# Cross attentions of two decoder layers without the identity products that TensorE ran in their gaps

## The chip, the cores and the metric

The kernel runs on one core of a Trainium2 chip. The metric is the device time of one execution in microseconds. A core has five engines that run side by side and meet at semaphores: TensorE (matrix products into PSUM; its weight loads are a lane of their own in the profile), VectorE, ScalarE, GpSimd and SyncE (which issues the DMAs). TensorE's clock is granted at one of two levels, 2.4 and 1.2 GHz; the profile shows it as a share, 1.00 or 0.50.

## The reference, cut to what matters

The program is a decoder of four layers, each with a mixing sublayer, a cross attention and a feed-forward sublayer, on x of 4 sequences x 512 tokens x 128. The two layers in question have the same cross attention, with 16 heads of width 8 over a context of 77 rows:

```python
q = query @ Wq.T + bq                      # query = layernorm(x)
k = key @ Wk.T + bk                        # key = value = context, 77 rows
v = value @ Wv.T + bv
attn = einsum('bhqd,bhkd->bhqk', q, k) / sqrt(8)
attn = softmax(attn, axis=-1)
out = einsum('bhqk,bhkd->bhqd', attn, v)
x = x + (out @ Wo.T + bo)
```

## The kernel before, in words

A loop of two passes takes two sequences each. A pass has twelve stages in a fixed order (`STAGES`), each run for the first sequence and then for the second, every one a block of its own in which each engine has a written-out list of instructions; engines meet at the block's end. So the cross attention is built four times (`stage_l0_xattn`, `stage_l1_xattn`, two sequences each) and executed eight times. Layer 0's follows a linear attention and is followed by an expert layer (`experts_stage` with weighed outputs); layer 1's follows a causal attention and is followed by another expert layer. While a stage works on one sequence it also does pieces of the norm of the other one (`m.side`): adding the last result to the residual, mean and variance on VectorE, a transpose on TensorE.

`cross_attention_stage` for one sequence: TensorE makes keys (L609), queries (L610) and values (L611). ScalarE adds biases, VectorE spreads the keys over four head groups. The score products (L624) come in four groups of 128 tokens, four row quarters of the array at a time; VectorE takes the maximum of each group (L715), and from the third on a score group waits for the banks that a maximum has freed. The negated maxima, split into two bf16 parts, are transposed on TensorE (L631), copied by ScalarE (L681), and added to scores made anew the other way round: per head group g, `shifted(g)` makes products of keys and queries (L640) and adds the shift (L645), ScalarE takes the exponential of all of it (L686), and `mix(g)` multiplies with the values and with ones (L654). TensorE's order is shifted(0), shifted(1), mix(0), shifted(2), mix(1), shifted(3), mix(2), the side's transpose, mix(3). VectorE then takes the reciprocals of the sums (L730) and multiplies (L732), in two halves, and TensorE projects each half (L671).

In five places of this list TensorE runs identity products before it waits: `m.warm(pe, count, bank)` multiplies the bf16 identity with four copies of itself (L97, 128x128 by 128x512) into a bank that nothing has yet to read. These are six before the scores, ten before the transposes of the maxima, ten before shifted(1), ten before the first half of the projection, four before the second: 40 in a stage. Other stages have such products of their own (the expert layer of layer 0 has 36 before its gates are transposed).

Of the kernel before, what the change touches and what calls it, by code (L numbers as in the profile page):

```python
# [560 lines left out]
def cross_attention_stage(m, name, w):  # L561
# [6 lines left out]
    with ExitStack() as ctx:  # L568
# [33 lines left out]
        with nc.Block(no_gpsimd_drain=True) as block:  # L602
            @block.sync
            def _(sync):
                m.housekeeping(sync)

            @block.tensor
            def _(pe):
                pe.matmul(m.psum[:, 5, 0:S2], w["wk"], m.ctxT[:, :], start=True, stop=True).then_inc(qkv_psum, 1)  # L609
                pe.matmul(m.bank(4), w["wq"], m.xnT[:, :], start=True, stop=True).then_inc(qkv_psum, 1)  # L610
                pe.matmul(m.psum[0:S2, 6, 0:D], m.ctxT[:, :], w["wv"], start=True,  # L611
                          stop=True).then_inc(qkv_psum, 1)
                m.warm(pe, 6, 0)
                pe.wait_ge(q_ready, 1)
                pe.wait_ge(k_of_ready, 1)
                for t in range(NT):
                    base = 4 * (t % 2)
                    if t == 1:
                        pe.wait_ge(v_ready, 2)
                        m.side.released(pe)  # L620
                    if t >= 2:
                        pe.wait_ge(peak_ready, t - 1)
                    for r in range(R):
                        ins = pe.matmul(m.psum[:, base + r, 0:G * S2], qT[quad(r), t * P:(t + 1) * P],  # L624
                                        k_of[quad(r), :, :].rearrange("p g s -> p (g s)"), start=True, stop=True)
                    ins.then_inc(scores_ready, 1)
                pe.wait_ge(peak_ready, NT - 1)
                m.warm(pe, 10, 0)
                pe.wait_ge(shift_ready, 1)
                for t in range(NT):  # L630
                    ins = pe.transpose(m.psum[:, 4, t * P:(t + 1) * P],  # L631
                                       shift[:, t, :, :].rearrange("p r w -> p (r w)"), m.ident)
                ins.then_inc(shift_psum, 1)

                def shifted(g):
                    if g >= 1:
                        m.warm(pe, 10 if g == 1 else 0, 4)
                        pe.wait_ge(exps_ready, g)
                    for r in range(R):
                        pe.matmul(m.psum[0:S2, r, :], k_of[quad(r), g, :], qT[quad(r), :], start=True, stop=False)  # L640
                    if g == 0:
                        pe.wait_ge(shiftT_ready, 1)
                        pe.wait_ge(cleared, 2)
                    for r in range(R):
                        ins = pe.matmul(m.psum[0:S2, r, :], pick[quad(r), g, :], shiftT[quad(r), :], start=False,  # L645
                                        stop=True)
                    ins.then_inc(shifted_psum, 1)

                def mix(g):
                    pe.wait_ge(exps_ready, g + 1)  # L650
                    for n in range(2):
                        for r in range(R):
                            lhsT = v[:, 4 * r + g, :] if n == 0 else m.const["ones_of"][0:S2, g, :]
                            ins = pe.matmul(m.psum[quad(r), 5 + n, :], lhsT, prob[:, g % 2, r, :], start=g == 0,  # L654
                                            stop=g == G - 1, skip_group_check=True)
                    ins.then_inc(group_mixed, 1)

                for g in range(G + 1):
                    if g < G:
                        shifted(g)  # L660
                    if g >= 1:
                        mix(g - 1)
                    if g == G - 1:
                        pe.wait_ge(peak_ready, NT)
                        m.side.turn(pe, [m.psum[:, OUT, t * P:(t + 1) * P] for t in range(NT)])
                for half in range(2):
                    m.warm(pe, 4 if half else 10, 4)
                    pe.wait_ge(mixed_ready, half + 1)
                    m.side.taken(pe)
                    for t in (2 * half, 2 * half + 1):  # L670
                        pe.matmul(m.psum[:, OUT, t * P:(t + 1) * P], mixed[:, t * P:(t + 1) * P], w["wo"],  # L671
                                  start=t == 0, stop=True, skip_group_check=True)
# [3207 lines left out]
```

## Time and profile before

| | us |
|---|---|
| median of three executions | 4097.55 (4093.26 to 4102.58) |
| the profiled execution | 4104.73 |
| its span, first to last instruction | 4103.0 |
| TensorE busy with products, in the span | 3673.0 (90%), 37500 of them |
| identity products among them (L97) | 1304, busy 323.2 |
| VectorE busy | 2470.9 (60%) |
| ScalarE busy | 1540.4 (38%) |
| mean granted clock of TensorE | 0.957 |

Matmuls are pipelined and overlap in the rows, so that ten of them can take less time than ten times the duration of one. A row of the timeline has the start, the time taken, the engine (PE is TensorE's products, PEld its weight loads, DVE is VectorE, ACT is ScalarE), the line of the kernel, the operation, what it writes and reads, the shape, the count, and in brackets the idle time before it and what ended it. f32 products are listed twice each.

### The profile page before, as it was taken

Reading aid. Unit: us, or ns where it says so; the run is one execution under the profiler, and the core shown is the slowest. Engines: PE = TensorE matmul, PEld = TensorE weight load, DVE = VectorE, ACT = ScalarE, POOL = GpSimd, SP = SyncE. Lnnn points to the kernel's source line nnn. Section 1 sums busy time; section 2 is a strip of 40 time slices with the busy share of each in tenths; the row PEclk is TensorE's granted clock in tenths of the full one; section 3 lists DMA queues with packets and bytes.
Section 4 is the critical chain, followed back from the end, with each engine's and each line's share of the span. In section 5 each row is a group of like instructions: output and inputs, shape, how many; then the busy total and the mean of one; then the engine's idle time right before and its main releaser. Section 6 shows DMA issues by size and latency. Waiting matters only on the chain. (4 is left out here: it accounts for less than half of the span.)

```text
span 4103.0 us, 93379 instructions
## 1 busy us (share of the span) xinstructions
PE 3673.0 (90%) x37500; PEld 2356.3 (57%) x37500; DVE 2470.9 (60%) x5994; ACT 1540.4 (38%) x3558; POOL 883.9 (22%) x1564
## 2 busy tenths in 40 slices
PE   6998999988898889999979989999888988999999
PEld 3886886433354336665548868864333544466655
DVE  6677676566435676555466676765665356765454
ACT  4445444233222335432244454432332222345322
POOL 1441441011001203320024414410110011133100
PEclk9999999999999999899989999999999999989999
DMA  2000000010000000010010000000100000000100
GB/s 95 3 3 2 3 3 13 1 54 1 21 1 20 1 25 2 1 41 18 12 35 3 3 1 3 3 13 1 54 1 21 1 20 1 26 1 1 41 29 6
DMA packets 8676, 59.92 MB, mean 15 GB/s; under 512 B 893, under 2 KB 5297, under 8 KB 5937
## 3 DMA queue, kind: packets, MB, share of 16 engines
q1 hardware_dynamic: 8240, 53.86, 3.4%
q8 instruction: 304, 4.98, 0.5%
q14 instruction: 132, 1.07, 0.1%
HBM read 52.81 MB, written 1.05 MB: 13 GB/s over the span
## 5 line engine op out<-in xcount | busy, mean ns | idle before, releaser
L97 PE MATMUL psum<-ident_bf 128*128 128x512 bf16 x1304 | 323.2, 393 | 15.3 <-PEq L2566 4.0
L3113 ACT ACTIVATE l_attn_ax<-psum 128x128 f32<-128x128 f32 (+1 forms) x768 | 186.4, 278 | 397.0 <-PE psum L2928 276.8
L3352 DVE TENSOR_TENSOR l_attn_xx<-l_attn_xx,psum 128x256 f32<-128x256 f32 x512 | 205.0, 419 | 214.2 <-PE psum L2947 203.1
L438 ACT ACTIVATE l_ffn_silu<-psum 128x512 f32<-128x512 f32 (+2 forms) x208 | 124.1, 597 | 469.5 <-PE psum L404 415.0
L503 DVE TENSOR_TENSOR l_ffn_hidden<-l_ffn_silu,psum 128x512 f32<-128x512 f32 (+2 forms) x176 | 120.5, 687 | 283.6 <-ACT l_ffn_silu L438 283.6
L103 PEld LDWEIGHTS psum<-streamed_weights,l_ffn_hidden 128*128 128x128 f32 (+2 forms) x1664 | 215.4, 192 | 123.0 <-issue 112.3
L2943 PE MATMUL psum<-l_attn_ax,l_attn_xx 64*64 64x64 f32 x5120 | 272.0, 226 | 0.0
L2947 PE MATMUL psum<-l_attn_xx,l_attn_ax 64*64 64x64 f32 x5120 | 263.9, 223 | 0.0
L3239 POOL TENSOR_TENSOR l_attn_part<-l_attn_ab,streamed_weights 128x128 f32<-128x128 f32 x640 | 245.4, 414 | 39.4 <-PE psum L2928 20.3
L103 PE MATMUL psum<-streamed_weights,l_ffn_hidden 128*128 128x128 f32 (+2 forms) x1664 | 224.2, 278 | 14.1 <-DVE l_ffn_hidden L503 9.2
L97 PEld LDWEIGHTS psum<-ident_bf 128*128 128x128 bf16 x1304 | 126.3, 103 | 183.0 <-issue 50.1
L2943 PEld LDWEIGHTS psum<-l_attn_ax,l_attn_xx 64*64 64x64 f32 x5120 | 211.3, 140 | 17.7 <-issue 10.2
L2928 PE MATMUL psum<-l_attn_xx,l_attn_part 64*64 64x64 f32 x5120 | 205.7, 231 | 8.1 <-DVE l_attn_xx L3352 6.3
L936 DVE TENSOR_REDUCE l_attn_peak<-psum 128x4 f32<-128x2048 f32 (+3 forms) x128 | 182.6, 1484 | 47.0 <-PE psum L862 46.6
L2947 PEld LDWEIGHTS psum<-l_attn_xx,l_attn_ax 64*64 64x64 f32 x5120 | 210.5, 139 | 0.0
L2928 PEld LDWEIGHTS psum<-l_attn_xx,l_attn_part 64*64 64x64 f32 x5120 | 183.8, 142 | 36.6 <-issue 17.4
L904 ACT ACTIVATE l_attn_prob<-psum 128x1024 f32<-128x1024 f32 (+1 forms) x192 | 159.9, 882 | 76.9 <-DVE l_attn_total L946 42.4
L859 PE MATMUL psum<-l_attn_k,l_attn_q 32*128 32x512 f32 (+3 forms) x1024 | 117.2, 530 | 71.5 <-DVE l_attn_peak L936 57.7
L2721 DVE SCALAR_TENSOR_TENSOR l_attn_conv<-psum,streamed_weights,l_attn_conv 128x511 f32<-128x511 f32 (+2 forms) x192 | 140.7, 747 | 16.3 <-ACT l_attn_conv L2661 11.8
L403 PE MATMUL psum<-l_ffn_gated_x,streamed_weights 128*128 128x512 f32 x256 | 139.3, 626 | 5.9 <-DVE l_ffn_gated_x L482 5.9
L3218 POOL TENSOR_TENSOR l_attn_pm<-l_attn_pm,w_const 128x256 f32<-128x256 f32 x128 | 93.0, 730 | 210.6 <-DVE l_attn_pm L3279 210.6
L813 PE MATMUL psum<-l_attn_q,l_attn_k 32*128 32x512 f32 (+3 forms) x1024 | 102.9, 473 | 38.2 <-ACT l_attn_prob L904 38.2
(541 smaller groups left out, 7858.7 us busy)
## 6 DMA issues: line engine op xcount, KB each, us to landing
streamed_weights<-pack_l_ffn SPq DMA_DIRECT2D x2, 5284.0 KB, 15.3
streamed_weights<-pack_l_attn SPq DMA_DIRECT2D x3, 2848.5 KB, 9.6
streamed_weights<-pack_l_ffn SPq DMA_DIRECT2D x2, 3972.0 KB, 13.0
streamed_weights<-pack_l_xattn SPq DMA_DIRECT2D x2, 2496.0 KB, 9.4
streamed_weights<-pack_l_ffn SPq DMA_DIRECT2D x2, 2192.0 KB, 8.1
streamed_weights<-pack_l_xattn SPq DMA_DIRECT2D x2, 2048.0 KB, 8.8
streamed_weights<-pack_l_ffn SPq DMA_DIRECT2D x2, 1923.0 KB, 7.9
streamed_weights<-pack_l_attn SPq DMA_DIRECT2D x2, 1091.5 KB, 5.1
```

The source lines that it names most:

```text
L97: pe.matmul(self.bank(bank), self.ident_bf[:, :], self.ident_bf[:, :].unsqueeze(1).to_broadcast([P, NT, P]), start=True, stop=True)
L103: ins = pe.matmul(self.psum[:, OUT, t * P:(t + 1) * P], features[:, t * P:(t + 1) * P], weight, start=first and t == 0, stop=last, skip_gr ...
L403: pe.matmul(m.bank(n % 2)[0:r], w["up"][:, c:c + r], rhs, start=True, stop=True)
L904: act.activation(prob[:, u % SLOTS, 2 * half:2 * half + 2, 0:used(part)], m.psum[:, base:base + 2, 0:used(part)], ACT.Exp).then_inc(exps_r ...
L936: dve.tensor_reduce(peak[:, g, i, :], m.psum[:, base:base + R, 0:(i + 1) * P], AX, ALU.max, negate=True).then_inc(peak_ready, 1)
L2721: ins = dve.scalar_tensor_tensor(out=later, in0=m.psum[:, chunk_bank(n), 0:T - 3 + i], scalar=w["conv_w"][:, ORDER[n], i:i + 1], in1=later ...
L2928: ins = pe.matmul(m.psum[b, p, W * i:W * i + W], part[b, (M * n + l - 1) % 2, p, i, :], xx[b, n % 2, p, X, i, :], start=True, stop=True)
L2943: pe.matmul(m.psum[b, p, P + W * i:P + W * i + W], xx[b, n % 2, p, XT, i, :], ax[b, p, i, :], start=True, stop=True)
L2947: ins = pe.matmul(m.psum[b, p, 256 + W * i:256 + W * i + W], ax[b, p, i, :], xx[b, n % 2, p, XT, i, :], start=True, stop=True)
L3113: act.activation(ax[b, p, :, :], m.psum[b, p, 0:P].rearrange("p (i t) -> p i t", i=2), ACT.Copy).then_inc(ax_ready, 1)
L3239: pool.tensor_tensor(part[:, q % 2, p, :, :], ab[:, n % 2, p, :, 0:W], over_block(w["levels"][:, l, :]), ALU.mult).then_inc(part_ready, 1)
L3352: dve.tensor_tensor(both, both, m.psum[:, p, P:384], ALU.subtract).then_inc(x_less, 1)
```

## The change

Four calls of `warm` go from `cross_attention_stage`, which stand for five groups of products in each stage (the last call is in a loop of two). All other instructions, their order and their waits stay. The identity products of the other stages stay.

```diff
                 pe.matmul(m.psum[0:S2, 6, 0:D], m.ctxT[:, :], w["wv"], start=True,
                           stop=True).then_inc(qkv_psum, 1)
-                m.warm(pe, 6, 0)
                 pe.wait_ge(q_ready, 1)
                 pe.wait_ge(k_of_ready, 1)
...
                 pe.wait_ge(peak_ready, NT - 1)
-                m.warm(pe, 10, 0)
                 pe.wait_ge(shift_ready, 1)
...
                 def shifted(g):
                     if g >= 1:
-                        m.warm(pe, 10 if g == 1 else 0, 4)
                         pe.wait_ge(exps_ready, g)
...
                 for half in range(2):
-                    m.warm(pe, 4 if half else 10, 4)
                     pe.wait_ge(mixed_ready, half + 1)
                     m.side.taken(pe)
```

## Rows read from the trace of the kernel before

**Rows 1.** Head of the page.

```profile
span 4103.0 us, 93379 instructions
```

**Rows 2.** Stretches, L97 alone: from:to us, PE and PEld busy (count), clock, DMA.

```profile
715.10:748.30 33.20, 10.95 (x40) 4.03 (x40) 0.95 0.00 0
...
3117.30:3149.10 31.80, 9.48 (x40) 3.66 (x40) 1.00 0.01 1
```

**Rows 3.** Timeline of TensorE's two lanes, layer 0, second sequence, first pass.

```profile
716.48 1.46 PE L97 MATMUL psum<-ident_bf 128*128 128x512 bf16 x6
717.87 0.83 PEld L624 LDWEIGHTS psum<-l_xattn_k_of,l_xattn_qT 32*128 32x128 f32 x16 [0.42 <-issue]
722.93 3.80 PE L97 MATMUL psum<-ident_bf 128*128 128x512 bf16 x10 [0.55 <-DVE l_xattn_peak L715]
726.35 0.58 PEld L631 LDWEIGHTS psum<-w_const,l_xattn_shift 128*128 128x128 f32 x4
730.60 0.23 PEld L640 LDWEIGHTS psum<-l_xattn_qT,l_xattn_k_of 32*77 32x77 f32 x8 [0.42 <-ACT l_xattn_prob L686]
747.24 0.71 PE L671 MATMUL psum<-w_l_xattn,l_xattn_mixed 128*128 128x128 f32 x4 [0.55 <-DVE l_xattn_mixed L732]
```

**Rows 4.** Timeline of ScalarE and VectorE in the same stage.

```profile
716.46 0.69 ACT L679 ACTIVATE l_xattn_qT<-psum,w_l_xattn 128x512 f32<-128x512 f32 x1 [0.58 <-PE psum L610]
...
724.59 0.22 DVE L723 TENSOR_TENSOR l_xattn_shift<-l_xattn_peak,l_xattn_coarse 128x64 f32<-128x64 f32 x1
...
728.45 1.87 ACT L686 ACTIVATE l_xattn_prob<-psum 77x2048 f32<-77x2048 f32 x1 [0.65 <-PE psum L645]
731.96 1.87 ACT L686 ACTIVATE l_xattn_prob<-psum 77x2048 f32<-77x2048 f32 x1 [1.64 <-PE psum L645]
```

**Rows 5.** Stretches, TensorE: from:to us, PE busy (count), clock, DMA.

```profile
719.20:722.40 3.20, 1.60 (x16) 1.00 0.00 0
722.60:725.90 3.30, 2.97 (x8) 0.50 0.00 0
...
730.60:742.70 12.10, 11.87 (x105) 1.00 0.00 0
...
865.90:876.10 10.20, 9.91 (x61) 0.50 0.01 2
```

**Rows 6.** Timeline, begin of layer 1's stage, first sequence, first pass.

```profile
1039.29 0.42 PE L609 MATMUL psum<-ctxT,w_l_xattn 128*128 128x77 f32 x2 [0.42 <-PEq L792]
...
1043.74 1.32 PE L624 MATMUL psum<-l_xattn_k_of,l_xattn_qT 32*128 32x308 f32 x16
...
1041.15 0.69 ACT L679 ACTIVATE l_xattn_qT<-psum,w_l_xattn 128x512 f32<-128x512 f32 x1 [1.08 <-PE psum L610]
```

**Rows 7.** Timeline of TensorE in the causal attention, clock at either level.

```profile
864.44 1.14 PE L859 MATMUL psum<-l_attn_k,l_attn_q 32*128 32x512 f32 x8 [3.02 <-PEq L1000]
...
871.38 2.09 PE L859 MATMUL psum<-l_attn_k,l_attn_q 32*128 32x512 f32 x8
...
893.37 1.97 PE L800 MATMUL psum<-w_const,l_attn_shift 128*128 128x128 f32 x8 [0.30 <-DVE l_attn_peak L936]
...
897.19 0.66 PE L800 MATMUL psum<-w_const,l_attn_shift 128*128 128x128 f32 x4
```

**Rows 8.** Timeline, layer 0, first sequence: what precedes the first exponentials.

```profile
694.08 1.28 ACT L686 ACT_TABLE_LOAD   x1
694.11 0.12 PEld L645 LDWEIGHTS psum<-l_xattn_shiftT,l_xattn_pick 32*77 32x77 bf16 x4 [0.53 <-ACT l_xattn_shiftT L681]
694.28 0.39 PE L645 MATMUL psum<-l_xattn_shiftT,l_xattn_pick 32*77 32x512 bf16 x4
```

**Rows 9.** Timeline, begin of the expert layers after the second sequences.

```profile
752.47 8.31 PE L97 MATMUL psum<-ident_bf 128*128 128x512 bf16 x36
...
759.38 0.36 DVE L475 TENSOR_TENSOR l_ffn_gate<-l_ffn_work,l_ffn_parts 128x192 f32<-128x192 f32 x1
...
1111.74 1.13 PE L103 MATMUL psum<-streamed_weights,l_ffn_hidden 128*128 128x128 f32 x8 [0.91 <-DVE l_ffn_hidden L503]
```

## The prediction, made before the changed kernel was run

> **What bounds the kernel now.** I read the page first: 4103.0 us from first to last instruction [rows 1]; the profiled execution took 4104.73 us, so 1.73 us lie around the span, and it stands 7.2 us above the median of the runs, 4097.55. Then I read the eight cross attentions that the change touches: two layers, two sequences each, in a loop of two passes. I call them A1 and A2 (layer 0, first and second sequence), B1 and B2 (layer 1). Each takes about 33.3 us and issues 40 products of the identity with itself (L97), 320 in all [rows 2]; in A2 they fill 10.95 of 33.2 us of TensorE.
>
> The timelines of TensorE, VectorE and ScalarE over A2 show what each of the five groups stands in front of [rows 3, 4]. Group 1 (six) stands before the score products: the queries are there at 717.15 (716.46 plus 0.69), the scores' first weight load comes at 717.87. Group 2 (ten) stands before the transposes: the shifts are there at 724.81, the transposes' load comes at 726.35. Group 3 (ten) stands before the second head group: the first exponentials end at 730.32, the load comes at 730.60. Groups 4 and 5 (ten and four) stand before the two halves of the output projection; the row at 747.24 has an idle 0.55 us before it that VectorE's division ended, so there VectorE sets the time and the products cost nothing.
>
> So in each stage one chain runs through queries, scores, four maxima on VectorE, transposes, ScalarE's exponentials, mixing, reciprocals. TensorE lies on it in short pieces, and how long these take depends on the granted clock. That is the last view: stretches with the clock. In the mixing loop the clock is at 2.4 GHz (1.00), TensorE busy 11.87 of 12.10 us [rows 5]. In A2 it fell to 1.2 GHz (0.50) right after the later score groups, when TensorE had been busy 1.60 of 3.20 us, and was back while group 2 ran [rows 5]. Five of the eight stages show that fall in the middle; both B1 show one at their begin instead; the last B2 shows none and is 31.8 us long, about 1.5 us shorter than A2 [rows 2].
>
> **What goes, by the waits alone.** A released weight load follows within 0.05 us: in A1 at 694.11, where ScalarE, done with what it waited for, had gone on at 694.08 [rows 8].
> - Group 1: 717.87 less 717.20 is 0.67 us; alike in six stages. In B1, where the group ran at 1.2 GHz, the scores come at 1043.74 and the queries were there at 1041.84 [rows 6]: 1.86, and 1.92 in the second pass. Together 7.8 us.
> - Group 2: 726.35 less 724.87 is 1.48 in A2 (twice); the same difference is 0.94 and 0.91 in A1, 1.60 in the first B2, and nothing in the three stages where the group ran at full clock. Together 6.4 us.
> - Group 3: ScalarE waits 1.64 us between first and second exponentials [rows 4] and 1.41 between the later ones: 0.23 in six stages, nothing in A1, where an activation table is loaded before the first exponentials [rows 8]. Together 1.4 us.
> - Groups 4 and 5: nothing.
>
> The sum is 15.6 us, if nothing else changes.
>
> **What it costs.** The groups are the only work of TensorE in these gaps. Without them A2 has, after its first two score groups, two groups of 0.8 us, then 2.5 us idle (722.38 to 724.87), then transposes and first shifted scores, then 1.9 us idle until the exponentials are through. The clock fell already after 719.2 to 722.4, where the score groups stand with gaps of 1.04 and 0.55 us; what follows them after the change is emptier. So I take it that transposes and shifted scores run at 1.2 GHz in every stage, and that the mixing loop begins so. At the end, with two gaps (2.35 us from 742.77 to 745.12, and 1.4) around four short products, I take the clock to fall too, and the next stage to begin at 1.2 GHz.
>
> Prices, from rows at either level [rows 7]: eight score products of 512 columns take 1.14 us at 2.4 GHz and 2.09 at 1.2; four transposes 0.66, against 0.99 (1.97 for eight); ten identity products 3.80, most of them at half clock [rows 3], against 2.33 at full clock in the same stage.
> - Transposes to first exponentials: 2.10 us now (726.35 to 728.45). Colder by 0.33 for the transposes, 0.95 for L640, and about 0.37 for L645 (0.39 at full clock): 1.65 us in six stages, 9.9. In A1 the table load ends at 695.36, 0.7 us after L645 (694.67), and hides that much [rows 8]: 0.95 twice, 1.9.
> - Mixing loop: at full clock TensorE has 0.2 us to spare in 12.1, so it is the bound as soon as its work doubles, and a cold stretch costs half its length. Stretches at 1.2 GHz are from 3.3 us (722.6 to 725.9) to 10.2 (865.9 to 876.1) long [rows 5]. I take 4.7 us, nearer to the short one, as the loop leaves TensorE no idle time once it is the bound: 2.35 us times eight, 18.8. Bounds 1.7 and 5.1 each, 13 and 41 together.
> - Begin of A2 and B2: L609 and L610 to the queries take 2.04 us at full clock and 2.55 in B1, where the clock fell soon after the begin [rows 6]; at half clock throughout up to 3.3. So 0.5 to 1.3 more; I take 1.0, and 0.6 for the first score group (0.87 from its load to the first maximum): 1.6 times four, 6.4. In B1, cold already, 0.6 twice, 1.2.
> - Maxima: a later score group, 0.8 us, takes about 1.4 at half clock, which just fits under a maximum of that length; 0.15 in each stage, 1.2.
> - The second half of the projection at half clock, on the way to the stage's end: 0.71 becomes 1.05, by the transposes' ratio, as these are products of 128 columns too; eight times, 2.8.
> - The expert layers that follow A2 and B2 begin colder. In the first the 36 identity products that stay end after the gates are ready (752.47 plus 8.31 is 760.78; the gates end at 759.74 [rows 9]), so a delay there shows: 0.8 twice. In the second TensorE has 0.91 us of idle before its first down projection [rows 9], against some 4 us of products that slow down: 1.7 twice. Together 5.0; bounds nothing and 10.
>
> The costs make 9.9 + 1.9 + 18.8 + 6.4 + 1.2 + 1.2 + 2.8 + 5.0 = 47.2 us; less 15.6 is 31.6 us slower. On the profiled execution that is 4136.3; on the median of the runs **4129 us**.
>
> Nothing is added or moved: no DMA, no wait, no buffer. The banks that the groups wrote (0 and 4) are written again from a fresh start by what follows.
>
> **A rule of the skill, against the rows.** The clock fell in A2 after gaps of 1.04 and 0.55 us between bursts, not after a long idle stretch. The Trainium skill (TensorE: Matmul & The Clock Gate, "Why this matters for your kernels") asks only that no long idle gap stand between bursts of matmuls, and none of the gaps that stay here is as long as it names. By that rule the clock would not fall and the change would give the 15.6 us; it is the first rival, and the rows of five stages speak against it.
>
> **Rivals.**
> - Waits alone (12 in 100; the other side): the clock stays at 2.4 GHz, or falls only where it falls now. Its place is the gap before the transposes, its price the 15.6 us: 4082 us. For it: the last B2, where the clock never fell [rows 2]. Against it: there too the score groups ended in identity products, which now go. It decides if the clock at the transposes is 1.00 in most stages.
> - A short fall (12 in 100): the clock falls before the transposes, is back before the mixing loop, and stages begin at full clock. Then 9.9 + 1.9 + 1.2 stand against 15.6: 2.6 faster, 4095, that is no change. For it: in A2 it was back after 3.3 us. Against it: it came back under dense identity products, and now the exponentials leave TensorE idle there.
> - A long fall (14 in 100): the loop, which keeps the clock at 2.4 GHz now, doesn't soon bring it back once it begins at 1.2. One more stretch of 3.4 us per loop adds 8 times 1.7: 4143; the whole loop at half clock costs some 11.9 us in place of 2.35: 8 times 9.5 more, 4205. For it: 865.9 to 876.1, 9.91 of 10.20 us busy and still at 0.50.
>
> **How the numbers follow.** My forecast has 62 in 100; its own range is 4112 to 4150: down by 6 for the loop's lower bound and by some 11 for the stage begins and expert layers, up by 22 for the loop's upper one. With the rivals the range is 4092 to 4160: waits alone lies below, the worst of the long fall above. A change of under 0.2% (8 us) can't be told from none here. Faster by more: 0.15 (waits alone, part of the short fall); the same: 0.10; slower: 0.75.
>
> **What would show it.** Right: in the changed profile the clock is 0.50 from before the transposes into the mixing loop in nearly every stage; L640's eight products near 2 us there; exponentials one to two 1.5 us later than 1.41; A2 and B2 begin at 0.50; each stage some 3 to 5 us longer. Scores start 0.05 us after the queries and transposes 0.05 us after the shifts, whatever the clock. Wrong: the clock 1.00 through the loop and stages of about 31 us; or all the loss after the stages, in the expert layers, which I price lowest.

## The result, and the profile after

The changed kernel took 4142.34 us (median of three executions, 4142.20 to 4143.18), the kernel before, beside it, 4100.07: a ratio of 1.0105, with a 95% interval of 1.0085 to 1.0125. A fourth execution took 9095.90 us, at a mean granted clock of 1.00; it is left out of these figures, and nothing here shows its cause. A second comparison gave 1.0077 (1.0059 to 1.0094): 4141.26 against 4110.29. The two differ in the kernel before (4100.07 and 4110.29), hardly in the changed one. The change makes the kernel slower by some 31 to 43 us. The forecast was 31.6 slower, 4129 us with a range of 4112 to 4150; the measured time lies in that range, in its upper part.

The heads of the page after: span [rows 1], busy time of the engines, and the identity products that are left.

```profile
span 4141.5 us, 92747 instructions
...
PE 3655.9 (88%) x37180; PEld 2338.9 (56%) x37180; DVE 2473.0 (60%) x5994; ACT 1539.5 (37%) x3558; POOL 883.8 (21%) x1564
...
L97 PE MATMUL psum<-ident_bf 128*128 128x512 bf16 x984 | 238.7, 387 | 11.9 <-PEq L2562 4.0
```

The span is 38.5 us longer, with 320 products fewer. I cut both traces at the first instruction of each stage (VectorE's addition to the residual) to see where. The eight cross-attention stages are 31.7 us longer together (3.4 to 5.7 each), the four expert layers that follow A2 and B2, in their first sequence, 11.1 (2.0 twice, 2.7, 4.4), and all the rest is 4.3 shorter, in pieces of up to 3 us of either sign in stages that nothing was changed in. One part of that rest is regular: the second sequences of the same expert layers are 1.6 to 1.9 us shorter each, 6.8 together, so that the expert layers as a whole lose 4.3.

Within A2 the granted clock answers to [rows 2, 5]. TensorE's stretches after the change: from:to us, length, PE busy (count), clock, DMA share, GB/s.

```profile
689.30:706.30 17.00, 12.51 (x60) 0.50 0.00 0
...
716.60:723.40 6.80, 4.80 (x15) 0.50 0.00 0
723.50:730.10 6.60, 2.44 (x32) 1.00 0.00 0
730.30:733.60 3.30, 3.21 (x16) 0.50 0.00 0
733.70:737.00 3.30, 1.52 (x16) 1.00 0.00 0
737.10:743.80 6.70, 6.70 (x36) 0.50 0.01 2
743.90:754.00 10.10, 7.37 (x64) 1.00 0.00 0
754.20:764.30 10.10, 8.86 (x22) 0.50 0.00 0
```

The first row is A1, from the transposes into the mixing loop; the others run through A2, from before its begin to the expert layer. In A2 the clock is at 1.2 GHz four times: over the begin, at the transposes, inside the loop, and at the end. Ahead of the last three falls TensorE had stood idle for part of a stretch at 2.4 GHz: it was busy 2.44 of 6.60 us, 1.52 of 3.30, 7.37 of 10.10. The loop, which ran at full clock from its first product [rows 5], spends 6.7 us at half.

TensorE's timeline over A2 [rows 3] shows what that makes of the instructions: start us, us, line, operands, count, and the idle time before with what ended it.

```profile
717.83 1.22 PE L667 MATMUL psum<-w_l_xattn,l_xattn_mixed 128*128 128x128 f32 x4 [1.41 <-DVE l_xattn_mixed L728]
...
719.94 2.00 PE L610 MATMUL psum<-xnT,w_l_xattn 128*128 128x512 f32 x2
...
722.72 1.62 PE L623 MATMUL psum<-l_xattn_k_of,l_xattn_qT 32*128 32x308 f32 x16 [0.35 <-ACT l_xattn_qT L675]
...
730.13 1.02 PE L629 MATMUL psum<-w_const,l_xattn_shift 128*128 128x128 f32 x4 [2.58 <-DVE l_xattn_shift L719]
731.08 2.00 PE L637 MATMUL psum<-l_xattn_qT,l_xattn_k_of 32*77 32x512 f32 x8
...
735.48 1.10 PE L637 MATMUL psum<-l_xattn_qT,l_xattn_k_of 32*77 32x512 f32 x8 [1.97 <-ACT l_xattn_prob L682]
...
738.15 1.95 PE L651 MATMUL psum<-l_xattn_prob,w_const 77*32 77x512 f32 x8
740.03 2.00 PE L637 MATMUL psum<-l_xattn_qT,l_xattn_k_of 32*77 32x512 f32 x8
...
744.95 1.10 PE L637 MATMUL psum<-l_xattn_qT,l_xattn_k_of 32*77 32x512 f32 x8
```

The same eight shifted scores (L637) take 2.00, 1.10, 2.00 and 1.10 us, by the clock alone. The first pair of waits is gone as forecast: the scores start 0.05 us after the queries (721.98 plus 0.69 is 722.67).

ScalarE's exponentials, four a stage [rows 4, 8]; the first two rows are the second and third of A1, the rest the first three of A2.

```profile
699.72 1.87 ACT L682 ACTIVATE l_xattn_prob<-psum 77x2048 f32<-77x2048 f32 x1 [2.53 <-PE psum L642]
705.65 1.87 ACT L682 ACTIVATE l_xattn_prob<-psum 77x2048 f32<-77x2048 f32 x1 [4.06 <-PE psum L642]
...
733.55 1.87 ACT L682 ACTIVATE l_xattn_prob<-psum 77x2048 f32<-77x2048 f32 x1 [1.77 <-PE psum L642]
736.83 1.87 ACT L682 ACTIVATE l_xattn_prob<-psum 77x2048 f32<-77x2048 f32 x1 [1.41 <-PE psum L642]
742.50 1.87 ACT L682 ACTIVATE l_xattn_prob<-psum 77x2048 f32<-77x2048 f32 x1 [3.80 <-PE psum L642]
```

The number in brackets is the wait for TensorE: 1.41 us at full clock. In A2 it is the third exponentials that come late, 2.39 us later than at full clock, not the second. So it is in B1, where the third wait 3.74:

```profile
1067.87 1.87 ACT L682 ACTIVATE l_xattn_prob<-psum 77x2048 f32<-77x2048 f32 x1 [1.41 <-PE psum L642]
1073.48 1.87 ACT L682 ACTIVATE l_xattn_prob<-psum 77x2048 f32<-77x2048 f32 x1 [3.74 <-PE psum L642]
```

The expert layer behind A2 [rows 9], TensorE's timeline after:

```profile
758.45 1.97 PE L403 MATMUL psum<-xnT,streamed_weights 128*64 128x512 f32 x2
...
762.06 9.06 PE L97 MATMUL psum<-ident_bf 128*128 128x512 bf16 x36
```

The stage begins with the residual's addition, at 748.37 us before and 756.67 after. Its 36 identity products end 12.41 us after that before, 14.45 now: 2.04 later, which is all that this stage lost (2.04 us). They start 1.29 us later, behind projections at half clock, and take 0.75 longer. In the second sequence of this layer it goes the other way. The same products, before and after:

```profile
795.30 9.07 PE L97 MATMUL psum<-ident_bf 128*128 128x512 bf16 x36
...
805.01 8.07 PE L97 MATMUL psum<-ident_bf 128*128 128x512 bf16 x36
```

They take 1.00 us less, and the mean granted clock over that stage is 0.96 for 0.92 before.

### The profile page after: what moved, and what is told of

The parts are those of the page before. It is cut to its first block and busy times, and to the rows that moved or that the text cites. A ratio compares the mean times of both kernels' runs of the same rounds, so it can differ in the third digit from the quotient of the medians.

```text
span 4141.5 us, 92747 instructions
## 1 busy us (share of the span) xinstructions
PE 3655.9 (88%) x37180; PEld 2338.9 (56%) x37180; DVE 2473.0 (60%) x5994; ACT 1539.5 (37%) x3558; POOL 883.8 (21%) x1564
## 3 DMA queue, kind: packets, MB, share of 16 engines
HBM read 52.81 MB, written 1.05 MB: 13 GB/s over the span
## 5 line engine op out<-in xcount | busy, mean ns | idle before, releaser
L97 PE MATMUL psum<-ident_bf 128*128 128x512 bf16 x984 | 238.7, 387 | 11.9 <-PEq L2562 4.0
L103 PE MATMUL psum<-streamed_weights,l_ffn_hidden 128*128 128x128 f32 (+2 forms) x1664 | 223.7, 277 | 12.3 <-DVE l_ffn_hidden L503 7.3
L97 PEld LDWEIGHTS psum<-ident_bf 128*128 128x128 bf16 x984 | 94.8, 102 | 130.4 <-issue 29.5
```

The costliest lines, as they stand in the source:

```text
L97: pe.matmul(self.bank(bank), self.ident_bf[:, :], self.ident_bf[:, :].unsqueeze(1).to_broadcast([P, NT, P]), start=True, stop=True)
L103: ins = pe.matmul(self.psum[:, OUT, t * P:(t + 1) * P], features[:, t * P:(t + 1) * P], weight, start=first and t == 0, stop=last, skip_gr ...
```

## The experiments

The theory: the groups do no work that the result needs, but they keep TensorE busy, and without them the granted clock falls before the transposes, in the loop and at the ends. Its rivals: that the waits alone count (each group costs time, or nothing), and that the loss lies in the order of the queue and not in the clock. Executions of the kernel before lie between 4093 and 4117 us. In its one profiled execution the two passes' cross-attention stages agree to about 0.05 us, all but B2 (33.50 and 31.80). So for each run I give the ratio, and beside it the sum over the eight stages against the profile of before, which shows where the time went. Such a sum rests on one profiled execution of each kernel; the two of the changed kernel differ by 5.9 us.

**Group 1 alone taken out.**

```
-                m.warm(pe, 6, 0)
```

> Group 1 alone goes (six products before the scores). Clock theory: groups 2 to 5 still raise the clock, so only the wait goes: scores 0.67 us earlier in A1, A2 and B2 (six stages), some 1.3 in B1, where the group ran at half clock; 5 to 8 us faster in all, mixing loops at 1.00. Rival, that the products help by being in TensorE's queue (weight loads pulled ahead, no start-up after a wait): each group is worth its share, and a fifth of the loss of the whole change, some 8 us, comes back.

Measured: 0.997 (0.9954 to 0.9986). The stages are 8.1 us shorter, 6.3 of it between their begin and the first maximum, 1.7 in sum between the shifts and the first exponentials. The 1.7 is the clock's doing and no wait: group 2 now runs at full clock in A2 and the first B2 (1.5 and 1.7 us sooner), and at half for longer in A1 and B1 (0.5 and 0.9 later). In sum group 1 only costs. By the ratio the kernel gained 12.3 us, some 4 more than its stages. The profiled execution was the fastest of seven, and its span 21.5 us shorter than before; 13.6 of these lie in one stage that nothing was changed in, in both passes. That stage in the first pass, before and in this run (from:to us, length, PE busy (count), clock, DMA share, GB/s):

```profile
1531.00:1675.40 144.40, 133.04 (x1042) 0.91 0.05 19
...
1523.60:1661.30 137.70, 125.90 (x1042) 0.96 0.05 20
```

So that part too is the clock, 0.96 for 0.91; why it fell less there, no run shows.

**Group 2 alone taken out.**

```
-                m.warm(pe, 10, 0)
```

> Group 2 alone goes (ten before the transposes). Clock theory: transposes and the first L640 run at 1.2 GHz in nearly all stages, 1.4 us lost against the waits of 1.48, 0.94 and 1.60 that go in the five stages where the clock fell anyway, so nothing there and 1.5 lost in the other three; group 3 then runs partly at half clock and ends after the first exponentials, about 1.5 in six stages, but brings the clock back before the loop: 8 to 15 us slower. Rival, that the fall before the transposes is what costs the loop its clock: loops at 0.50 for a stretch, 25 to 30 us slower.

Measured: 0.9998 (0.9988 to 1.0007). The stages are 9.8 us longer, in the expected range, but the kernel's time is not: the rest gave 4.5 back in the profiled execution. The 9.8 are 3.8 between the shifts and the first exponentials and 6.2 between the first and the second, less small parts. TensorE's timeline of this kernel in A2 shows both:

```profile
728.49 2.00 PE L639 MATMUL psum<-l_xattn_qT,l_xattn_k_of 32*77 32x512 f32 x8
730.27 0.65 PE L644 MATMUL psum<-l_xattn_shiftT,l_xattn_pick 32*77 32x512 bf16 x4
730.85 2.78 PE L97 MATMUL psum<-ident_bf 128*128 128x512 bf16 x10
733.56 1.10 PE L639 MATMUL psum<-l_xattn_qT,l_xattn_k_of 32*77 32x512 f32 x8
```

The clock fell before the transposes, and group 3 brought it back, itself partly at half clock, so that it ended late (2.78 us for 2.33). Behind it the loop ran at full clock. The rival, a loss of 25 to 30, is refuted.

**Group 3 alone taken out.**

```
-                        m.warm(pe, 10 if g == 1 else 0, 4)
```

> Group 3 alone goes (ten between L645 and the second L640). Clock theory, as the changed kernel's trace shows it: TensorE waits 1.9 us for the first exponentials (3.2 in A1), the clock falls after that wait and the loop runs at 0.50 for up to 6.8 us: 2.7 us lost in a stage, 15 to 24 us slower in all. Rival, that the fall before the transposes alone decides: group 2 still prevents it, the loop stays at 1.00, and the kernel is 1.4 us faster.

Measured: 0.9986 (0.9977 to 0.9996). A miss: I expected a slower kernel, and it came out some 6 us faster, nearer to the rival. The stages are 3.8 us longer in sum. In two of the eight the clock fell in the loop (2.9 us each); it stayed at 2.4 GHz in the loops of the other six. In the six stages outside A1 the second exponentials came 0.23 us sooner. The wait in A1 is 2.63 us here, and 1.97 in the changed kernel, not the 3.2 that I had written. TensorE in one that fell, A1:

```profile
697.22 1.10 PE L639 MATMUL psum<-l_xattn_qT,l_xattn_k_of 32*77 32x512 f32 x8 [2.63 <-ACT l_xattn_prob L685]
...
701.99 2.01 PE L639 MATMUL psum<-l_xattn_qT,l_xattn_k_of 32*77 32x512 f32 x8
```

So the loop's fall isn't group 3's alone to prevent: with group 2 in place it happened in two stages of eight.

**Groups 4 and 5 taken out.**

```
-                    m.warm(pe, 4 if half else 10, 4)
```

> Groups 4 and 5 go (fourteen at the two halves of the projection). Clock theory: the second half takes 1.2 in place of 0.7 us (4 us over eight stages), A2 and B2 begin at 0.50 as B1 does now (1.7 us later at the first maximum, 7 in all), and the expert layers after A2 and B2 lose 2.0 and 2.7 or more (10 in all): 18 to 22 us slower, less what later stages give back. Rival, that VectorE sets the time there and the next stage's own products raise the clock at once: no change, within 4 us.

Measured: 1.0021 (1.0011 to 1.0031), 8.7 us, less than half of what was expected. The rival, no change, falls too: it had the next stage's products raise the clock at once. The stage begins lost 7.9 us and the ends 3.9, about as expected, but shifts to first exponentials took 5.5 us less, so that the stages are 6.2 longer. The expert layers lost 6.9 in their first sequence, 10 by the expectation, and gained 3.5 in the second. TensorE's timeline around the begin of A2:

```profile
713.96 1.22 PE L670 MATMUL psum<-w_l_xattn,l_xattn_mixed 128*128 128x128 f32 x4 [1.30 <-DVE l_xattn_mixed L731]
...
716.08 2.00 PE L610 MATMUL psum<-xnT,w_l_xattn 128*128 128x512 f32 x2
...
725.17 2.33 PE L97 MATMUL psum<-ident_bf 128*128 128x512 bf16 x10 [0.55 <-DVE l_xattn_peak L714]
```

The projection's second half and the queries run at half clock, and group 2 then at full: 2.33 us, where it took 3.80 before [rows 3]. A fall moved to the begin spares one in the middle.

The four ratios alone add up to −0.0025, some 10 us faster; all four edits at once, which is the change, made 31 to 43 us slower. Part of that distance lies in stages that nothing touches, as in the run without group 1. In the cross-attention stages the four add up to 11.7 us longer (−8.1, +9.8, +3.8 and +6.2), against 25.8 and 31.7 with the change. The groups cover for each other either way, and the next runs take pairs.

**Groups 2 and 3 taken out** (both edits above).

> Groups 2 and 3 both go; 1, 4 and 5 stay. Clock theory with an interaction: either group alone brings or keeps the clock up before the mixing loop, so each alone cost the loop little; without both the loop starts at 1.2 GHz or falls there after the first exponentials, and the third exponentials come 5.6 us or more after the second in nearly all stages: some 2.7 us in each loop, stages together 22 to 26 us longer, the kernel 18 to 28 us slower. Rival, that the groups' effects simply add: stages 13.6 us longer (9.8 and 3.8 measured apart) and the kernel, by the medians apart, some 7 us faster.

Measured: 1.0047 (1.0029 to 1.0064), some 19 us slower. The stages are 19.6 us longer; 9.8 and 3.8 would make 13.6. Between first and fourth exponentials 16.1 us are lost, against 6.2 and 4.5 for one group alone. The stages stay a little under what I expected, the total is in its range. That the parts add up is refuted: by them the kernel would be 7 us faster. The profiled execution is the fastest of four here too (4108.52; the others 4123 to 4128), and has a clock of 0.96 in the stage shown under group 1.

**All five groups kept, with products of 8 columns in place of 512.**

```
+    def narrow(self, pe, count, bank=OUT):
+        for _ in range(count):
+            pe.matmul(self.psum[:, bank, 0:8], self.ident_bf[:, :], self.ident_bf[:, 0:8], start=True, stop=True)
...
-                m.warm(pe, 6, 0)
+                m.narrow(pe, 6, 0)
```

and the same in the other four places.

> All 40 products of a stage stay, each with 8 columns in place of 512. Clock theory: they keep TensorE's queue as it was but not its array busy, so clock and time are those of the change: stages 29 to 34 us longer together, the kernel 35 to 45 us slower. Rival, that it is the instructions in the queue that help (weight loads ahead, no restart after a wait): the kernel within 4 us of before or faster, since short products end sooner.

Measured: 1.0053 (1.0036 to 1.007), some 22 us slower. The rival, within 4 us, is refuted; my 35 to 45 us were too many. The stages are 24.1 us longer, where I expected 29 to 34, since the loop stayed at 2.4 GHz in both A2 stages. TensorE's timeline in A1 of this kernel:

```profile
691.09 0.43 PE L103 MATMUL psum<-ident_bf 128*128 128x8 bf16 x10 [0.55 <-DVE l_xattn_peak L720]
693.02 1.11 PE L636 MATMUL psum<-w_const,l_xattn_shift 128*128 128x128 f32 x4 [1.50 <-DVE l_xattn_shift L728]
694.07 2.00 PE L645 MATMUL psum<-l_xattn_qT,l_xattn_k_of 32*77 32x512 f32 x8
...
698.47 2.00 PE L645 MATMUL psum<-l_xattn_qT,l_xattn_k_of 32*77 32x512 f32 x8 [1.61 <-ACT l_xattn_prob L691]
```

The number of instructions and their order are those of before, TensorE is idle 1.50 us before the transposes, and the stages lose all but 2 to 8 us of what they lost with the change (25.8 and 31.7 us in its two profiled executions). So nearly all of it is what the products fill, and not their place in the queue.

**The change, with group 3 put back.** (Diff: groups 1, 2, 4 and 5 out, as above.)

> The change, with group 3 put back (groups 1, 2, 4, 5 go). Clock theory: group 3 raises the clock before the second head group, so the loop runs at 1.00 from there (24 us back), but its ten products run partly at half clock and delay the second exponentials by 0.5 to 1.5 us in a stage (8 lost); stage begins and expert layers lose as in the change: 20 to 26 us slower than before. Rival, that the clock falls again in the loop whatever stands before it: 38 us or more slower, as in the change.

Measured: 1.0036 (1.0022 to 1.0051), some 15 us slower where I expected 20 to 26; the stages are 14.7 us longer. In every stage the clock is back at 1.00 from the second head group on. TensorE in B2, first pass, where group 3 itself still runs mostly at half clock:

```profile
1093.90 3.60 PE L97 MATMUL psum<-ident_bf 128*128 128x512 bf16 x10
1097.43 1.10 PE L638 MATMUL psum<-l_xattn_qT,l_xattn_k_of 32*77 32x512 f32 x8
```

One group in that place leaves 6.0 us lost between first and fourth exponentials; the change lost 24.0 there in its first profile, and 18.2 in its second.

**The change, with groups 4 and 5 put back.** (Diff: groups 1, 2 and 3 out.)

> The change with groups 4 and 5 put back (1, 2, 3 go). Clock theory: stages begin and the expert layers run as before (there the change lost 11 us), transposes and loops run as with groups 2 and 3 gone (19.6 us) less 6 to 8 for the scores that come sooner: stages 11 to 15 us longer, the kernel 4 to 16 us slower. Rival, that the groups in the middle carry nearly all the loss: 28 us slower or more, the change less the 8.7 us that the end groups were worth alone.

Measured: 1.004 (1.0028 to 1.0052), 16 us, at the upper edge of what was expected; the stages, 16.3 longer, lie just above. The begins are 6.2 us shorter than before, the ends unchanged, the expert layers within 1.1; what is left is the loop, 18.3, and 4.0 before it. So groups 4 and 5 decide the begins, the projection's end and the expert layers. They don't hold the loop, which loses as much as in the second profile of the change; but they move its fall. In A2 and B2 it is now the second head group that runs at half clock, its scores taking 2.00 us, and the third at full.

**The change, run again** (no edit).

> The change itself once more, timed beside the runs of before on the chip that the two others of this call use. Clock theory: the eight stages are again some 31 to 33 us longer, to a tenth of a microsecond alike in each stage's begin; the kernel 32 to 44 us slower, the spread coming from where in the rest of the kernel the clock falls. Rival, that the first ratio owed much to few runs of before: under 25 us.

Measured: 1.0077, given above, 31 us slower, just under what I expected. The stages are 25.8 us longer in this profiled execution, not 31 to 33: 5.9 less than in the first. Both B2 loops stayed at full clock this time, as ScalarE's rows in the first B2 show:

```profile
1105.77 1.87 ACT L682 ACTIVATE l_xattn_prob<-psum 77x2048 f32<-77x2048 f32 x1 [1.41 <-PE psum L642]
1109.05 1.87 ACT L682 ACTIVATE l_xattn_prob<-psum 77x2048 f32<-77x2048 f32 x1 [1.41 <-PE psum L642]
```

Whether a loop falls in the changed kernel can differ from one execution to the next. The total doesn't show it: these two profiled executions took 4143.18 and 4143.03 us, so the rest of the kernel took up what B2 gave back. The distance between 1.0077 and 1.0105 lies in the kernel before, so the rival had a point: the first ratio owed some 10 us to the few executions of before beside it.

**Fewer products instead of none.** Group 1 out, group 2 shortened to eight, group 3 to nine, groups 4 and 5 kept.

```
-                m.warm(pe, 6, 0)
...
-                m.warm(pe, 10, 0)
+                m.warm(pe, 8, 0)
...
-                        m.warm(pe, 10 if g == 1 else 0, 4)
+                        m.warm(pe, 9 if g == 1 else 0, 4)
```

> A version to beat both: group 1 goes, group 2 has eight and group 3 nine products, 4 and 5 stay. Clock theory: 8 us in the stages from group 1 as measured apart; in the four stages where group 2 runs at half clock it ends 0.85 us sooner, 3.4; the second exponentials come 0.2 us sooner in six stages, 1.3; loops stay at 1.00: 13 us from the stages, the kernel 12 to 20 us faster than before. Rival, that two products fewer are enough to let the clock stay down before the loop: loops at 0.50 in A1 and B1, no faster than without group 1 alone or slower than before.

Measured: 0.9956 (0.9941 to 0.997), 4088.51 us, in the expected range; the stages are 10.8 us shorter, every loop at full clock. **The same with six in group 2:**

```
-                m.warm(pe, 10, 0)
+                m.warm(pe, 6, 0)
```

> As the version with fewer products (no group 1, nine in group 3), but six in group 2 in place of eight. Clock theory: where group 2 runs at half clock (A1 and B1) it ends another 0.85 us sooner, 3.4 in all, if the clock is still back by the second head group because of group 3: 18 to 24 us faster than before. Rival, that six are too few: the transposes and L640 run at 0.50 (1.4 us lost in those stages) and the second exponentials come later than 3.5 us after the first: 8 to 16 us faster only.

Measured: 0.9941 (0.9924 to 0.9958), 4086.43 us, the lowest median here, though its interval overlaps that of the version with eight. The stages are 13.5 us shorter: 6.3 at the begin, 5.5 between shifts and first exponentials (of which 1.7 had come with group 1's going alone), 1.3 in the loop. TensorE in its A1, first the timeline, then two stretches with the clock:

```profile
690.72 2.74 PE L97 MATMUL psum<-ident_bf 128*128 128x512 bf16 x6 [0.55 <-DVE l_xattn_peak L714]
693.25 0.79 PE L630 MATMUL psum<-w_const,l_xattn_shift 128*128 128x128 f32 x4
693.97 1.10 PE L639 MATMUL psum<-l_xattn_qT,l_xattn_k_of 32*77 32x512 f32 x8
695.21 2.12 PE L97 MATMUL psum<-ident_bf 128*128 128x512 bf16 x9
697.91 1.10 PE L639 MATMUL psum<-l_xattn_qT,l_xattn_k_of 32*77 32x512 f32 x8 [0.58 <-ACT l_xattn_prob L685]
```

```profile
690.70:693.50 2.80, 2.79 (x8) 0.50 0.00 0
694.00:710.30 16.30, 15.49 (x128) 1.00 0.00 1
```

The clock falls here too, before the transposes, but it does so under six identity products and is back when the shifted scores start. In A2 and B2 it doesn't fall there at all, and the six take 1.47 us.

## Why the prediction was right, point by point

- **That the change slows the kernel, by the clock: right.** Four falls stand in A2 where there was one, and narrow products, which leave the queue as it was, lose most of the time too. Waits alone, the rival of the other side, is refuted by the sign that it named: at the transposes the clock was at half in all eight stages (they took 1.02 to 1.09 us, 0.60 before). TensorE's longest wait in the stage's first part is 2.58 us, and the clock was at half behind it. So the rule of the Trainium skill (TensorE: Matmul & The Clock Gate, "Why this matters for your kernels"), which against such falls asks only for no long idle gap, doesn't cover this kernel; the measured rows decide.
- **The waits that go.** In the changed kernel the scores' first load follows the queries by 0.05 us in all eight stages, the transposes' follows the shifts by 0.12 (0.05 by the forecast). Group 1's 7.8 us came out at 6.3 in the run without it: 0.67 in six stages, as forecast, but 1.12 in B1 for 1.86 and 1.92. Group 2's 6.4 can't be measured by itself, as the clock falls without it; six products in place of ten, both without group 1, brought 3.8. Group 3's 0.23 in six stages: exact.
- **Transposes to first exponentials:** shifts to first exponentials came 3.9 us later in sum, 5.4 by the forecast (9.9 + 1.9 less 6.4). L640's products (now L637) take 2.00 us; "near 2" was the forecast.
- **Mixing loop: the term that was too small.** Between first and fourth exponentials the stages lost 24.0 us net, 17.4 by the forecast (18.8 less 1.4). With the waits of 1.4 that is 25.4, or 3.2 us a stage for 2.35, well inside the bounds of 1.7 to 5.1 (the second profile has 18.2 net, or 2.4 a stage). The cold stretch was longer, 6.7 us in A2 and 17.0 in A1 (which takes in the transposes), for the 4.7 that I took. And it was not the stretch I described. I had the loop begin cold, with the second exponentials late; in A2, and in both B stages of the first profile, the clock is back at 2.4 GHz when the first exponentials run, falls a second time behind that wait, and the third are late. Only A1 goes as I wrote. So that the term came out near its size is in part luck. "Short fall" had that return right, and missed the second fall. "Long fall" has a price, 4143, that fits the measured total better than mine, but not by its path: it asks for 4.05 us a loop, and part of the total lies in the expert layers and in the base.
- **Stage begins and projection:** A2 and B2 begin at 0.50, L610 takes 2.00 us. Begin to first maximum came out at nothing over all stages, −0.2 by the forecast; fourth exponentials to end +4.0, 2.8 by the forecast, as the second half takes 1.22 us and not 1.05. The maxima cost nothing, for 1.2.
- **Expert layers: 11.1 for 5.0** in the first sequences, which I had priced, just over the upper bound of 10. I left out that their second sequences would gain: 6.8 us, as a fall that stood there before was shorter or gone. Net it is 4.3, near my 5.0 for no reason of mine. The second layer's share was priced by 4 us of slowed products less 0.91 of idle time; it lost 2.7 and 4.4. In the first layer the path was right and the price not: the 36 products both start later and run longer, 2.0 for 0.8.
- **All the rest** was taken at nothing and, with those 6.8, gave 4.3 us back. This and the two terms above partly cancel; the forecast's closeness to the second comparison (31) owes something to that. The absolute 4129 is 13 us low, and most of that is its base: I added to the median of three executions, 4097.55, while later medians of the kernel before are 4108 to 4111.

What stays open: why the clock falls sometimes more and sometimes less in stages that nothing touches, as in the one that made the kernel without group 1 gain more than its stages did. I ran nothing that isolates it.

## What to carry to other kernels

Products that only keep TensorE busy can't be judged one by one: here the four edits, each alone, sum to 10 us faster (11.7 longer in the stages), and together they cost 31 to 43 (25.8 and 31.7 in the stages). Judge such a group by where the clock falls next without it, and then trim it until it ends with the wait that it stands in: a group whose absence costs the clock little goes (group 1, 8 us), and one in which the fall itself happens runs at half clock and so needs fewer products. In A1 without group 1, six took 2.74 us, where ten had taken 3.77:

```profile
688.83 3.77 PE L97 MATMUL psum<-ident_bf 128*128 128x512 bf16 x10 [0.55 <-DVE l_xattn_peak L714]
```

To tell the clock from the queue, make the products narrow: same instructions, next to no work.

## What the hardware showed that I had not expected

- In the loop of A2 the clock came back behind a stretch in which TensorE had been busy 3.21 of 3.30 us, at half speed, and fell again behind the next, busy 1.52 of 3.30; in A1 it stayed at 0.50 for 17.0 us, with TensorE busy 12.51 of them.
- A fall at one place can spare one later: with the begin of A2 at half clock, the ten products of group 2 ran at full clock, 2.33 us for 3.80; and in the first profile of the change, each expert layer that began at half clock had a second sequence 1.6 to 1.9 us shorter.
- Ten products of 8 columns, 0.43 us in all, did not bring the clock back before the transposes of A1 (1.11 us), where ten of 512 did (0.60).
- Of one and the same kernel, the changed one, an execution can have its B2 loops at full clock or not, 5.9 us apart in the stages and 0.15 us in the whole.
